# Row maxima turned by VectorE's 32x32 block transposes instead of by an identity product on TensorE, in a sliding-window attention and recurrent-gate kernel

## The reference, cut to what matters

```
q, k, v = split(x @ w_in.T)                      # 16 heads of 16
scores  = q.k/4 + slope[h]*(distance), masked to own and previous block of 128 tokens
o       = softmax(scores) @ v ; x1 = layernorm(x + o @ w_out.T)
for each sequence t:                              # c is the state, one per token row
    f, i, g = sigmoid/tanh(x1[t] @ w.T + c @ u.T + b)
    c = f*c + i*g
h   = tanh(x1 @ wo.T + c_final @ uo.T + bo) ; out = layernorm(x1 + h)
```

## Time and profile before

| what | value |
|---|---|
| runs of before | 1016.15 us median of 3 (1015.51 to 1016.79) |
| the profiled execution | 1015.92 us; its span, first to last instruction, 1014.1 us |
| PE busy | 914.6 us (90% of the span) |
| DVE busy | 712.1 us (70%) |
| ACT busy | 575.0 us (57%) |
| POOL busy | 396.1 us (39%) |
| mean granted TensorE clock | 0.951 of full speed |

### The profile page before, as it was taken

How to read it: one execution, slowest core, us unless ns; L and a number is a source line. 1 busy time by engine, 2 the same in 40 slices (tenths; PEclk the granted TensorE clock), 3 DMA queues, 4 the chain that set the end, 5 groups by cost and what they waited for, 6 DMA issues and landing times.

```text
span 1014.1 us, 25913 instructions
## 1 busy us (share of the span) xinstructions
PE 914.6 (90%) x9500; PEld 753.2 (74%) x9500; DVE 712.1 (70%) x2792; ACT 575.0 (57%) x1165; POOL 396.1 (39%) x679
## 2 busy tenths in 40 slices
PE   3287878999999999999999999999999989889994
PEld 2165666878788878788878787888788877678884
DVE  6356577787868686868787878787878673336885
ACT  5034446575757575756565656565656454425876
POOL 3023334353535353535353535353535352101343
PEclk9576889999999999999999999999999989899998
DMA  6554354444444544444444445444544400121764
GB/s 199 145 155 127 106 147 134 141 136 138 138 137 140 134 141 133 143 132 145 129 145 129 148 126 149 127 148 127 147 108 148 123 31 22 42 76 51 227 198 135
DMA packets 92958, 131.99 MB, mean 130 GB/s; under 512 B 12008, under 2 KB 46696, under 8 KB 92832
## 3 DMA queue, kind: packets, MB, share of 16 engines
q1 hardware_dynamic: 92832, 130.34, 44.3%
HBM read 78.84 MB, written 50.33 MB: 127 GB/s over the span
## 4 chain that ended last, share of the span: by engine, by line
PE 62%; DVE 24%; ACT 4%; issue 4%; SPq 2%; POOL 2%; DMA 1%; ACTq 0%; DVEq 0%; POOLq 0%
PE bank L919 29%; DVE bank L690 10%; PE bank L907 10%; PE bank L938 8%; PE bank L973 7%; PE bank L959 3%; DVE max_q L690 2%; PE bank L981 2%; DVE qk_parts L663 2%; DVE gate L739 2%; DVE gate L737 1%; PE bank L1014 1%; PE bank L1027 1%; ACT Pt L645 1%; DVE stats L875 1%
## 5 line engine op out<-in xcount | busy, mean ns | idle before, releaser
L690 DVE CUSTOM_DVE_ANT_0 bank<-bank,mask 128x256 f32<-128x256 f32 (+1 forms) x1024 | 368.9, 422 | 149.6 <-PE bank L938 148.3
L448 ACT ACTIVATE Pt<-bank 128x512 f32<-128x512 f32 (+1 forms) x512 | 248.1, 536 | 202.2 <-PE bank L959 202.0
L354 POOL TENSOR_SCALAR_AFFINE_SELECT Pt<-Pt 128x512 f32<-128x512 f32 x256 | 174.5, 682 | 446.7 <-ACT Pt L448 446.7
L938 PE MATMUL bank<-Ks,Qs 58*128 58x256 f32 (+1 forms) x1024 | 149.4, 319 | 61.5 <-DVE max_q L690 37.7
L938 PEld LDWEIGHTS bank<-Ks,Qs 58*128 58x128 f32 x1024 | 108.2, 192 | 105.1 <-DVE max_q L690 52.2
L690 DVE DVE_READ_ACCUMULATOR2_ANT max_q<- 128x1 f32 x1024 | 143.8, 140 | 0.0
L356 POOL TENSOR_SCALAR_AFFINE_SELECT Pt<-Pt 128x384 f32<-128x384 f32 x256 | 139.3, 544 | 0.0
L973 PE MATMUL bank<-Pt,Vp 128*32 128x256 f32 (+1 forms) x2048 | 131.5, 378 | 0.0
L919 PE MATMUL bank<-x1T,Wg 64*128 64x512 f32 x960 | 128.1, 398 | 0.8 <-DVE o_tok L704 0.8
L919 PE MATMUL bank<-cT,Ug 64*128 64x512 f32 x960 | 125.9, 393 | 0.0
L959 PE MATMUL bank<-Qs,Ks 59*128 59x256 f32 (+1 forms) x1024 | 111.7, 270 | 0.4 <-ACT Pt L448 0.3
(11 more groups left out here) (112 smaller groups left out, 1341.8 us busy)
## 6 DMA issues: line engine op xcount, KB each, us to landing
parts_dram<-qk_parts SPq DMA_DIRECT2D x128, 256.0 KB
Qs<-parts_dram SPq DMA_DIRECT2D x128, 128.0 KB, 2.6
Ks<-parts_dram SPq DMA_DIRECT2D x128, 128.0 KB, 2.7
xt_raw<-in_xt SPq DMA_DIRECT2D x16, 512.0 KB, 4.3
Qs<-parts_dram SPq DMA_DIRECT2D x128, 64.0 KB, 2.6
Ks<-parts_dram SPq DMA_DIRECT2D x128, 64.0 KB, 2.7
x_res<-in_x SPq DMA_DIRECT2D x16, 512.0 KB, 3.9
x_dram<-y SPq DMA_DIRECT2D x16, 512.0 KB, 3.8
```

Of the source, the lines that this page charges most:

```text
L354: gp.affine_select(out=p4[:, :, 0:128], in_=p4[:, :, 0:128], compare_op=ALU.is_ge, fill=0.0, base=0, pattern=[[0, 4], [1, 128]], channel_m ...
L448: sc.activation(probabilities(g, 2 * pair + odd)[:, S * a:S * a + n], SC[odd][:, 0:n], ACT.Exp).then_inc(exp_done, 1)
L690: ins = ve.tensor_tensor_reduce(out=raw, in0=raw, in1=mask[:, keys], scale=1.0, scalar=MASKED, op0=ALU.add, op1=ALU.max, accum_out=max_q[: ...
L938: ins = te.matmul(MX[odd][:, 256 * (n % 2):256 * (n % 2) + 256][:, keys], Qs[rows, 2 * g + pair, n * WIN:(n + 1) * WIN], Ks[rows, 2 * g + ...
```

## The change

PE's product with the identity and ACT's copy are gone. Instead DVE, directly after the last maxima of a group, transposes max_q in four blocks of 32 partitions by 32 columns into max_t, whose rows then hold the maxima of 128 queries. Both halves of max_q are widened to 32 columns and cleared once. There is no negation any more: the constant rows in Ks are -1 instead of 1. The DMAs into Qs read max_t. On PE the waits that went with max_transpose move to its neighbours, and two of them that named maxrow_done are replaced.

```diff
-        max_q = sb("max_q", [128, 2, 16])
-        max_rows = sb("max_rows", [16, 128], F32R)
+        max_q = sb("max_q", [128, 2, 32])
+        max_t = sb("max_t", [BLOCK, 2, 128])
...
 def max_to_stack(t, g):                                     # SP
-                wait(sp, maxrow_done, 4, t, g + 1)
+                wait(sp, mt_done, 4, t, g + 1)
...
-            def max_row(t, g, bank):                        # ACT, called four times an iteration
-                pt, pg = before(t, g)
-                wait(act, maxrow[pg], 16 * MAXROW_DMAS, pt, 16 * MAXROW_DMAS)
-                wait(act, mt_ready, 4, t, g + 1)
-                sc.activation(max_rows[:, :], bank[0:16, 0:128], ACT.Copy, scale=-1.0).then_inc(maxrow_done, 1)
...
             def maxima(t, g, s):                            # DVE
                 if s == 0:
-                    wait(dve, mt_ready, 4, t, g - 1)
+                    wait(dve, mt_done, 4, t, g - 1)
...
+            def max_transpose(t, g):                        # DVE
+                pt, pg = (t, g - 2) if g >= 2 else (t - 1, g + 2)
+                wait(dve, red_done, 32, t, 8 * g + 8)
+                wait(dve, maxrow[pg], 16 * MAXROW_DMAS, pt, 16 * MAXROW_DMAS)
+                for q in range(0, 128, BLOCK):
+                    ins = ve.transpose(max_t[:, g % 2, q:q + BLOCK], max_q[q:q + BLOCK, g % 2, :])
+                ins.then_inc(mt_done, 1)
...
                 def attend(slot):                           # DVE
                     maxima(t, slot // 4, slot % 4)
+                    if slot % 4 == 3: max_transpose(t, slot // 4)
...
+            ve.memset(max_q[:, :, :], 0.0).then_inc(max_cleared, 1)
-            ve.memset(Ks[:, :, :].bitcast(F32), 1.0).then_inc(mem_ready, 1)
+            ve.memset(Ks[:, :, :].bitcast(F32), -1.0).then_inc(mem_ready, 1)
...
-            def max_transpose(t, g, bank):                  # PE, called four times an iteration
-                wait(pe, red_done, 32, t, 8 * g + 8)
-                te.matmul(bank[0:16, 0:128], max_q[:, g % 2, :], ident[:, :], start=True, stop=True).then_inc(mt_ready, 1)
...
                 attend(8)                                   # PE, one of the four places
-                freed(pe, (qklo_done, 4, t + 1, 1), (y_done, 2, t - 2, 1))
-                max_transpose(t, 1, B0)
                 if p1:
                     freed(pe, (qklo_done, 4, t + 1, 2), (y_done, 2, t - 2, 2))
                     values(t - 1, 3, B1)
-                    wait(pe, maxrow_done, 4, t, 2)
+                    freed(pe, (qklo_done, 4, t + 1, 1), (y_done, 2, t - 2, 1))
                     ctx_transpose(t - 1, 2, B0)
```

More of the change, by code:

```diff
@@ L37 @@
 MAXROW_DMAS = 2
+BLOCK = 32
 POSROW_DMAS = 8
@@ L134, in build @@
         bias_ready = sem("bias_ready")
-        mx_ready, sc_ready, mt_ready, pv_ready, ct_ready, v_ready, qk_ready, ot_ready, op_ready, xt_ready, f_ready = (
-            sem(n) for n in ("mx_ready", "sc_ready", "mt_ready", "pv_ready", "ct_ready", "v_ready", "qk_ready",
+        mx_ready, sc_ready, max_cleared, pv_ready, ct_ready, v_ready, qk_ready, ot_ready, op_ready, xt_ready, f_ready = (
+            sem(n) for n in ("mx_ready", "sc_ready", "max_cleared", "pv_ready", "ct_ready", "v_ready", "qk_ready",
                              "ot_ready", "op_ready", "xt_ready", "f_ready"))
-        exp_done, ctx_done, maxrow_done, v_done, qkhi_done, othi_done, x1hi_done, gate_done, chi_done, xhi_done = (
-            sem(n) for n in ("exp_done", "ctx_done", "maxrow_done", "v_done", "qkhi_done", "othi_done", "x1hi_done",
+        exp_done, ctx_done, mt_done, v_done, qkhi_done, othi_done, x1hi_done, gate_done, chi_done, xhi_done = (
+            sem(n) for n in ("exp_done", "ctx_done", "mt_done", "v_done", "qkhi_done", "othi_done", "x1hi_done",
                              "gate_done", "chi_done", "xhi_done"))
@@ L268, in max_to_stack @@
             def max_to_stack(t, g):
-                wait(sp, maxrow_done, 4, t, g + 1)
+                wait(sp, mt_done, 4, t, g + 1)
                 for odd in range(2):
                     r = 64 * odd + ROW_MAX
-                    sp.dma_start(Qs[r:r + 1, 2 * g:2 * g + 2, :].bitcast(F32),
-                                 max_rows[8 * odd:8 * odd + 8, :].bitcast(F32)).then_inc(maxrow[g], 16)
+                    sp.dma_start(Qs[r:r + 1, 2 * g:2 * g + 2, :].bitcast(F32), max_t[8 * odd:8 * odd + 8, g % 2, :]).then_inc(maxrow[g], 16)
             def load_xt(t):
@@ L506, in iteration @@
                     gates(t - 3, 1, B1)
-                if p1: max_row(t - 1, 3, A0)
                 attend(0)
@@ L520, in iteration @@
                 if p3: gates(t - 3, 3, A1)
-                max_row(t, 0, A0)
                 attend(5)
@@ L531, in iteration @@
                     gates(t - 3, 5, A1)
-                max_row(t, 1, B0)
                 attend(8)
@@ L543, in iteration @@
                 if n1: qk_hi(t + 1, 2, B0)
-                max_row(t, 2, A0)
                 attend(13)
@@ L558, in last_sequences @@
                 gates(t - 2, 1, B1)
-                max_row(t, 3, A0)
                 exps(t, 2, 1)
@@ L854, in _ @@
                 minus_hi(cT[:, 1, j, :], c2[:, j, :], cT[:, 0, j, :]).then_inc(c0_lo, 1)
+            dve.wait_ge(max_cleared, 1)
             for t in range(B):
@@ L1070, in iteration @@
                 if p1:
-                    freed(pe, (x1lo_done, 2, t - 3, 1), (qklo_done, 4, t, 3))
-                    max_transpose(t - 1, 3, A0)
                     freed(pe, (x1lo_done, 2, t - 3, 2), (qklo_done, 4, t, 4))
                     values(t - 1, 1, A1)
-                    wait(pe, maxrow_done, 4, t - 1, 4)
+                    freed(pe, (x1lo_done, 2, t - 3, 1), (qklo_done, 4, t, 3))
                     ctx_transpose(t - 1, 0, A0)
@@ L1100, in iteration @@
                 attend(5)
-                freed(pe, (gate_done, 6, t - 3, 3), (o_done, 4, t - 1, 1), (qklo_done, 4, t, 3))
-                max_transpose(t, 0, A0)
                 if p1:
@@ L1105, in iteration @@
                     values(t - 1, 2, A1)
-                    wait(pe, maxrow_done, 4, t, 1)
+                    freed(pe, (gate_done, 6, t - 3, 3), (o_done, 4, t - 1, 1), (qklo_done, 4, t, 3))
                     ctx_transpose(t - 1, 1, A0)
                 if n1:
-                    freed(pe, (y_done, 2, t - 2, 1), (maxrow_done, 4, t - 1, 3), (qklo_done, 4, t, 1))
+                    freed(pe, (y_done, 2, t - 2, 1), (v_done, 2, t - 1, 1), (qklo_done, 4, t, 1))
                     project_qk(t + 1, 0, B0)
@@ L1133, in iteration @@
                 v0, v1 = v_halves(t, 0, A0), v_halves(t, 1, A1)
-                freed(pe, (gate_done, 6, t - 3, 5), (o_done, 4, t - 1, 2), (maxrow_done, 4, t, 1))
+                freed(pe, (gate_done, 6, t - 3, 5), (o_done, 4, t - 1, 2), (qklo_done, 4, t, 3))
                 freed(pe, (gate_done, 6, t - 3, 6), (ctx_done, 4, t - 1, 3), (qklo_done, 4, t, 4))
@@ L1142, in iteration @@
                     q2, q3 = qk_halves(t + 1, 2, B0), qk_halves(t + 1, 3, B1)
-                    freed(pe, (o_done, 4, t - 1, 3), (maxrow_done, 4, t, 2))
+                    freed(pe, (o_done, 4, t - 1, 3), (qklo_done, 4, t + 1, 1))
                     freed(pe, (ctx_done, 4, t - 1, 4), (qklo_done, 4, t + 1, 2))
@@ L1149, in iteration @@
                 attend(13)
-                wait(pe, v_done, 2, t, 1)
-                max_transpose(t, 2, A0)
                 values(t, 0, A1)
                 if p1:
-                    wait(pe, maxrow_done, 4, t, 3)
+                    wait(pe, v_done, 2, t, 1)
                     ctx_transpose(t - 1, 3, A0)
@@ L1183, in last_sequences @@
                 scores(t, 2, 1)
-                wait(pe, x1lo_done, 2, t - 2, 1)
-                max_transpose(t, 3, A0)
                 wait(pe, x1lo_done, 2, t - 2, 2)
                 values(t, 1, A1)
-                wait(pe, maxrow_done, 4, t, 4)
+                wait(pe, x1lo_done, 2, t - 2, 1)
                 ctx_transpose(t, 0, A0)
```

## The result

The changed kernel takes 1031.72 us (median of 4, 1030.77 to 1033.39) against 1016.47 of the kernel before (4 runs): ratio 1.0153, 95% interval 1.0135 to 1.0171, so 15.3 us or 1.5% slower. Slower was forecast, but half as much, and the time lies outside the range. It is the time of rival B, and not for B's reason, as the rows show.

The account below looks back on a forecast made before the run. PE sets the pace mostly, DVE in slots 7 to 9. Removal -7.9, slot 7 +12.1, slot 3 +2.7, early iterations and t = 15 +0.8 make +7.7: 1023.7 us, 0.75% slower; range 1015.5 to 1029 us.

Parts of the forecast that it names:

- rival B: A block transpose costs what RECIPROCAL does, about 0.25 us each: +15.2 us, 1031 us; chance 0.09.
- Where PE and DVE alternate: PE sets the pace mostly; DVE alone for 9.4 us in slots 7 to 9, in 13 iterations (t = 3 to 15).
- Rival D: The change costs nothing because DVE has idle time (30% of the span): -7.9 us, 1008 us; chance 0.02.
- The removal: PE's identity products on the chain, in full iterations in slots 5 and 0, give back 7.9 us; ACT's copies nothing.
- Four transposes end to end: On DVE at each group end, four block transposes do not overlap: 4 x 0.19 us.
- T: DVE time added per group end, read and wait plus transposes: 0.93 us; paid in full in slot 7, 13 x 0.93 = 12.1 us.
- Slot 3's excess: Group 0's end: 0.93 us against 0.72 us of DVE waiting leaves 0.21 us, 13 times: 2.7 us.
- An excess in slot 11 goes into that. Nothing: Group 2's end: 0.21 us excess goes into DVE's 0.94 us wait one slot later; otherwise another 2.7 us.
- the clock: PE's granted clock: no term in the sum; a different clock from PE idling 0.9 us more in slot 10 would make it wrong.
- the 1.9 us that I had expected: Sign in the changed profile: PE's two waits in slot 10 grow from 0.93 to about 1.9 us.
- the forecast's terms for the early iterations and the end: Slots 3 and 7 of t = 0 to 2 and slot 12 of t = 15: excess over waits, together 0.8 us.
- Rival C: L741's collision with GpSimd in slot 8 goes away, 1019.6 us (chance 0.08), or hits a second operation, 1027.7 us (0.04).

Follow-up runs that it names:

- e7: Changed kernel, but group 1 (transposes in slot 7) keeps the TensorE product and ScalarE copy; groups 0, 2, 3 on VectorE: 1016.66 us, ratio 0.9994.
- e4: Only group 3 (after slot 15) transposed on VectorE; groups 0 to 2 as in the kernel before, without the negation: 1013.41 us, ratio 0.9959.
- e1: Changed kernel without any transposes on VectorE; the DMAs wait for the last reduction and read a tile filled once: 1006.34 us, ratio 0.9906.
- e3: Changed kernel, but all four transposes read the block of partitions 0 to 31: 1026.19 us, ratio 1.0102.
- e5: Changed kernel plus five unused 128x512 products on TensorE in slot 9, t = 3 to 15, filling its wait: 1029.08 us, ratio 1.0128.
- e6: Changed kernel, but one 128x32 transpose instruction per group instead of four blocks, and four DMAs instead of two: 1021.8 us, ratio 1.0048.
- e8: Against the kernel before: groups 0 and 3 transposed on VectorE, one 128x32 instruction and four DMAs each; groups 1, 2 unchanged in path: 1009.87 us, ratio 0.9927.
- e2: Kernel before, product and copy kept, plus the wait and four block transposes per group end into an unread tile: 1038.17 us, ratio 1.0216.
- e9: Changed kernel with one 128x32 transpose and four DMAs per group, plus five unused TensorE products in slot 9, t = 3 to 15: 1012.37 us, ratio 0.9964.
- e10: Control: the kernel before plus five unused TensorE products in slot 9: 1015.54 us, ratio 0.9996.

## Why the prediction was wrong

**Where PE and DVE alternate: right.** Slots 7 to 9 are DVE's, L946 counts only in slots 5 and 0. e7 takes the whole loss away by moving one group; e4 shows a group end that costs nothing. Rival D is out.

**The removal: right in the iterations, and near in its total partly by luck.** The chain gave 0.42 us an iteration in slots 5 and 0; e1 shows 0.39 and the changed kernel the same. The totals, 7.9 us forecast and 9.4 us in e1, can't be set against each other as they are: e1 has 0.11 us an iteration from the missing wait and up to 2.75 us from the clock in t = 15.

**Four transposes end to end: right, and mis-sized.** The term 4 x 0.19 = 0.76 us measured 0.84, because each takes 200 ns and is followed by a gap of 0.013 us; with 0.18 for the read and the wait, and 0.03 behind them, T is 1.05 instead of 0.93: 1.6 us over 13 iterations. Both lie within what I had allowed for T, 0.81 to 1.05, whose upper end I had put at 1027.4 us; the mis-sized T alone does not leave the range. I gave the fill and drain as the reason why they cannot overlap. e3 shows that this is not the reason: from one quadrant they do. The rule of the Trainium skill that I had set beside it, "VectorE: DVE Perf Modes", section "Two Vector instructions with no wait between them" (another start quadrant than the last one holds an instruction until all earlier ones are done), agrees with e3 and with the changed kernel, 0.48 against 0.84 us. It covers the operation behind them as well, which starts 0.06 us before the end in e3 and 0.03 us after it in the changed kernel. Rival B is out: its total came out, its price of 0.25 us for a transpose did not.

**Slot 3's excess: right, and mis-sized.** 0.32 to 0.33 us instead of 0.21, all of it from T; 1.6 us more.

**"An excess in slot 11 goes into that. Nothing": not quite.** Of 0.32 us, 0.08 came through: about 1.0 us. I take it that PE's scores of slot 12 start later and with them ACT's exponentials and its copy for `qk_lo`; no run tests this way.

**What was missing: the clock.** This is the step that failed: the sum held PE's granted clock unchanged and had no term for it, though the last sentence had named it as what would make the prediction wrong. The runs show three drops in its place, worth 1.9 to 3.7 us. Without them the changed kernel takes 1029.1 us (e5; 1029.8 by its distance to the kernel before), about the end of the range (1029), which the mis-sized terms above and below had used up; the drops took it clear of the range. PE's wait in slot 10, in the profile of the changed kernel:

```profile
527.00 0.32 PE L938 MATMUL bank<-Ks,Qs 58*128 58x128 f32 x1 [0.89 <-DVE max_q L679]
527.76 0.38 PE L938 MATMUL bank<-Ks,Qs 58*128 58x128 f32 x2 [0.44 <-DVE max_q L679]
```

0.40 us more idle than before in each iteration went with 3.7 us lost in three of them, by the slots, and e5, which fills that wait, took 1.9 to 2.6 us off. The wait did not grow to the 1.9 us that I had expected, because another part of T reached PE earlier, over ACT: the gates wait for `update`, and the exponentials of slot 8 stand behind them in ACT's queue, so PE's scores of slot 9 are held up. From L938 in slot 9 to L919, the products behind the scores, PE needs 1.32 us instead of 0.58, and the profile counts all of it as busy. The kernel before, then the changed one:

```profile
515.46 0.51 PE L938 MATMUL bank<-Ks,Qs 58*128 58x256 f32 x4
516.04 1.58 PE L919 MATMUL bank<-Win,xT 64*128 64x256 f32 x24
...
523.09 0.82 PE L938 MATMUL bank<-Ks,Qs 58*128 58x256 f32 x4
524.41 1.70 PE L919 MATMUL bank<-Win,xT 64*128 64x256 f32 x24
```

And in the changed kernel ACT's gate and the wait of PE's weight loads for ACT:

```profile
522.10 0.69 ACT L480 ACTIVATE gate<-bank,bias_half 128x512 f32<-128x512 f32 x1 [1.26 <-DVE c L738]
...
524.18 0.29 PEld L955 LDWEIGHTS bank<-Qs,Ks 59*128 59x128 f32 x3 [0.20 <-ACT Pt L448]
```

The sum with measured terms: forecast +7.7, T +1.6, slot 3 +1.6, slot 11 +1.0, clock +1.9 to +3.7, makes 13.8 to 15.6, for 15.3 measured. So the excess over the forecast, 7.6 us, is for more than half T, in three places, and for the rest the clock. That this closes so well is partly luck, as it keeps the forecast's terms for the early iterations and the end. The two profiled executions, taken stretch by stretch, give 16.4 us between their spans: -0.63 up to the start of t = 3, +12.30 in the full iterations without drops, +3.68 for the three drops, +1.36 in t = 15 and -0.34 behind. **Rival C** did not happen: L741 (now L738) takes 819 ns in the mean against 818 before, and its collision with GpSimd moved along with it.

**What stays open.** Which wait brings a drop, and in which iteration. The first of the two waits in slot 10 is 0.89 us in the changed kernel and 0.88 in e3 and e6, all three with drops in the full iterations; it is 0.44 to 0.50 before and in e4, e7 and e8, 0.66 in e1 and 0.67 in e2, all without, and filled in e5 and e9, without too. But only 3 of the 12 full iterations drop in the changed kernel, 4 in e3 and 5 in e6, and e2's PE, which waits another 0.79 us in slot 8, has none. In t = 15 the kernel before and e4 have nearly the same waits of PE around slot 12, and the one drops and the other doesn't. No run here varied one wait in steps.

## What to carry to other kernels

Price an added operation by where it stands in its engine's queue, not by the engine's share: of four equal group ends one cost 1.05 us, one 0.32, one 0.08 and one nothing, and the best version puts work on VectorE at two of them only. A wait of TensorE has a second price if the clock falls after it; compare the granted clock in windows before blaming slots, and if it falls, products that nobody needs, laid into the wait, are a test of one edit. Four small transposes read from different 32-partition ranges ran strictly one after another here; one instruction over all partitions, with the rearranging left to DMAs that have time, took a quarter of the time. And before a gain of 2 or 3 us is believed, look in both profiles for a drop at one place: here one in the last iteration was worth up to 2.75 us.

## What the runs showed of the hardware that I had not expected

- A 128x32 block transpose takes 0.21 us, hardly more than a 32x32 one (0.20 us). Four from four quadrants take 0.84 us, four from one quadrant 0.48.
- A longer wait of PE at one place, 0.88 instead of 0.49 us before slot 10, in a stretch in which PE is busy for 96% (446.71 of 465 us), can cost more by the clock than a whole edit gives: e6 lost 8.4 to 9.4 us so.
- Adding 65 products of 128x512 made a kernel 8.4 to 9.4 us faster (e6 to e9), and another one no slower (e10).
- With nearly the same waits of PE, one execution had its clock at half from 825 to 832 us (the kernel before) and another had not (e4); the slot there took 7.7 and 5.2 us.
